# Choosing the experts of two routed layers in groups of 4 tiles, as their logits are moved, in place of 16 tiles at a time

## What is computed

```python
xn = _layernorm(x)
s = _L0_attn_ref(xn, ...)            # gated linear attention, 4 heads, chunks of 64
g = _silu(_L0_ffn_ref(xn, ...))      # 8 experts, the best 2 of a token
x = x + s * g
xn = _layernorm(x)
s = _L1_attn_ref(xn, ...)            # softmax attention, 16 heads
g = _silu(_L1_ffn_ref(xn, ...))      # 16 experts, the best 2 of a token
x = x + s * g
```

```python
# layer 0
gate_scores = softmax(x @ Wg.T)                       # [tokens, 8]
topk_val, topk_idx = top_k(gate_scores, 2)
topk_val = topk_val / (topk_val.sum(-1) + 1e-9)
# layer 1
scores = x @ router_w + router_bias                   # [tokens, 16]
topv, topi = top_k(scores, 2)
weights = softmax(topv)
```

## Time and profile before

| | |
|---|---|
| median of 3 runs | 1166.89 us (1165.84 to 1169.87) |
| the profiled execution, its own time | 1174.48 us |
| its span in the profile | 1172.5 us |
| mean granted TensorE clock | 0.83 |
| TensorE busy | 794.8 us, 68% |
| VectorE busy | 646.4 us, 55%, 1112 instructions |
| ScalarE busy | 625.9 us, 53%, 1093 instructions |
| GpSimd busy | 479.5 us, 41%, 486 instructions |
| the chain that ended last | PE 38%, DVE 19%, ACT 13%, unknown 11%, issue 10%, POOL 6% |

### The profile page before, as it was taken

One profiled execution on the slowest core, in us unless ns is written; L12 is line 12 of the kernel. 1 busy time (PEld: TensorE's weight loads), 2 busy tenths in 40 slices (PEclk: granted clock), 3 DMA queues, 4 the chain that ended last, 5 costly groups with the idle time before them and its releaser, 6 DMA issues.

```text
span 1172.5 us, 23626 instructions
## 1 busy us (share of the span) xinstructions
PE 794.8 (68%) x8916; PEld 620.2 (53%) x8916; DVE 646.4 (55%) x1112; ACT 625.9 (53%) x1093; POOL 479.5 (41%) x486
## 2 busy tenths in 40 slices
PE   5735668999999882477821028777988788788610
PEld 3424557888888762254610015455656566666510
DVE  7574336766765233977670016755656647465355
ACT  4433336768775311464500025667668778687722
POOL 3067542233432444520037730004346646555635
PEclk9667869999999997677955559989889999899855
DMA  9511111011011113300013111201001111010052
GB/s 325 190 45 55 52 39 45 21 34 34 29 34 33 47 47 111 78 1 2 1 29 147 52 43 37 73 19 29 20 28 38 35 31 38 28 38 29 19 152 72
DMA packets 62366, 63.92 MB, mean 55 GB/s; under 512 B 7378, under 2 KB 52322, under 8 KB 62132
## 3 DMA queue, kind: packets, MB, share of 16 engines
q1 hardware_dynamic: 53300, 43.99, 12.8%
q0 software_dynamic: 8960, 18.43, 4.8%
HBM read 31.84 MB, written 30.55 MB: 53 GB/s over the span
## 4 chain that ended last, share of the span: by engine, by line
PE 38%; DVE 19%; ACT 13%; another core or an unknown queue 11%; issue 10%; POOL 6%; DMA 2%; SPq 0%; POOLq 0%; ACTq 0%; DVEq 0%
PE bank L441 5%; POOL ys L1710 4%; PE bank L656 3%; ACT arena L1110 3%; PE bank L593 3%; DVE arena L1580 2%; ACT L804 2%; PE bank L595 2%; PE bank L607 2%; PE bank L481 2%; PE bank L594 2%; PE bank L721 2%; PE bank L621 1%; PE bank L367 1%
## 5 line engine op out<-in xcount | busy, mean ns | idle before, releaser
L1710 POOL DMA_INDIRECT ys<-arena x152 | 169.8, 1117 | 203.3 <-DVE arena L1472 86.0
L1110 ACT ACTIVATE arena<-bank 128x512 f32<-128x512 f32 x192 | 99.3, 600 | 137.2 <-remote 92.1
L1694 POOL DMA_INDIRECT xs<-arena x128 | 128.4, 1003 | 62.4 <-issue 36.5
L593 PE MATMUL bank<-arena 128*128 128x128 bf16 x608 | 139.2, 236 | 19.4 <-DVE arena L1453 7.4
L595 PE MATMUL bank<-arena 128*128 128x128 bf16 x608 | 138.8, 235 | 3.8 <-issue 3.8
L1580 DVE TENSOR_REDUCE arena<-bank 128x2 bf16<-128x512 f32 (+1 forms) x192 | 119.2, 683 | 40.2 <-remote 26.2
L594 PE MATMUL bank<-arena 128*128 128x128 bf16 x608 | 136.7, 232 | 3.9 <-issue 3.9
L804 ACT ACT_TABLE_LOAD x70 | 89.8, 1283 | 1.2
L593 PEld LDWEIGHTS bank<-arena 128*128 x608 | 63.3, 104 | 37.5 <-issue 28.5
L441 PE MATMUL bank<-arena 128*128 128x256 f32 x256 | 69.1, 424 | 18.4 <-DVE arena L1359 17.2
L679 PE MATMUL bank<-arena 32*128 32x256 bf16 (+1 forms) x512 | 22.3, 263 | 86.7 <-ACT arena L1110 61.2
(11 more groups left out here) (213 smaller groups left out, 2034.5 us busy)
## 6 DMA issues: line engine op xcount, KB each, us to landing
xs<-arena SPq DMA_DIRECT2D x19, 516.0 KB, 7.7
arena<-xs SPq DMA_DIRECT2D x38, 258.0 KB, 2.8
arena<-ys SPq DMA_DIRECT2D x32, 256.0 KB, 5.2
arena<-in_MF SPq DMA_DIRECT2D x8, 512.0 KB
ys<-arena POOLq DMA_INDIRECT x152
arena<-in_x SPq DMA_DIRECT2D x8, 256.0 KB, 5.6
arena<-in_W SPq DMA_DIRECT2D x8, 256.0 KB
xs<-arena POOLq DMA_INDIRECT x128
```

What stands on the lines that cost most here:

```text
L593: mm(o, hi, b[:, 0, c4], stop=False)
L1110: act(PT[kt_][:, i, gs[0]:gs[0] + len(gs), :], bank_of["s2", b, n, i][:, :].rearrange("p (g q) -> p g q", q=w), ACT.Exp, scale=8 ** -0.5). ...
L1694: eng.indirect_dma_start(xs[l][:, :], bass.IndirectOffsetOnAxis(ap=slot_i[l][:, m:m + 1], axis=0), xrow[:, t, :], None).then_inc(rows_move ...
L1710: eng.indirect_dma_start(ys[l][:, :], bass.IndirectOffsetOnAxis(ap=yid[g % 4][:, j:j + 1], axis=0), y[:, 128 * j:128 * j + 128], None).the ...
```

## The change

`choose` works on one group of 4 tiles instead of 16, and `logits_taken` calls it after each group's logits are moved, in both layers. The scratch `cand` and `ix` shrink with it, the waits of `route` go to the eighth choice, and `spread(h)` waits for the last of the four choices that it covers. The diff's first two parts are those waits on TensorE and ScalarE, the last one that on GpSimd.

```diff
@@ -396,7 +396,7 @@
-                eng.wait_ge(*chosen[l].at(1))
+                eng.wait_ge(*chosen[l].at(NG - 1))
@@ -840,14 +840,14 @@
-                eng.wait_ge(*chosen[0].at(h, 5))
+                eng.wait_ge(*chosen[0].at(4 * h + 3, 5))
...
-                eng.wait_ge(*chosen[l].at(1))
+                eng.wait_ge(*chosen[l].at(NG - 1))
@@ -1243,20 +1243,19 @@
                         tt(L.rearrange("p (t e) -> p t e", e=E), bank_of["logits", u][:, 0:n].rearrange("p (t e) -> p t e", e=E), bc(rb, 1, sh),
                            ALU.add).then_inc(l_moved.sem, 1)
-                    if h % 4 == 3:
-                        choose(l, h // 4)
+                    choose(l, h)
 
             def choose(l, h):
 
-                E, C, Z = EXPERTS[l], chosen[l], 16 * EXPERTS[l]
-                sh = [128, 16, E]
+                E, C, Z = EXPERTS[l], chosen[l], 4 * EXPERTS[l]
+                sh = [128, 4, E]
                 L3 = RS[l]["cu"][:, Z * h:Z * h + Z].rearrange("p (t e) -> p t e", e=E)
                 cand = RS[l]["to"][:, 0:Z].rearrange("p (t e) -> p t e", e=E)
-                ix = RS[l]["ix"][:, 0:16]
+                ix = RS[l]["ix"][:, 0:4]
                 Oem = one_hot[:, 0:64 * E].rearrange("p (e k t) -> p e k t", e=E, k=2)
-                tsh = slice(16 * h, 16 * h + 16)
+                tsh = slice(4 * h, 4 * h + 4)
                 rv = bc(rev[l], 1, sh)
-                eng.wait_ge(*l_moved.at(8 * l + 4 * h + 3))
+                eng.wait_ge(*l_moved.at(8 * l + h))
```

## The result

| | before | with the change |
|---|---|---|
| median, measured side by side | 1166.37 us (1161.17 to 1169.87, 4 runs) | 1186.19 us (1181.51 to 1187.93, 4 runs) |
| the profiled execution | 1174.48 us | 1181.51 us |
| its span | 1172.5 us | 1178.5 us |
| VectorE | 646.4 us, 1112 instructions | 664.9 us, 1250 instructions |
| TensorE | 794.8 us | 797.0 us |

The ratio is 1.0167, with a 95% interval of [1.0118, 1.0217]: slower, as forecast, but by 19.8 us (13.8 to 25.3) where 6.8 was forecast, and just outside the range of 1161 to 1185.

What follows compares the result with a forecast made beforehand. It took VectorE to become Layer 0's bound and small choices to delay waiting engines in Layer 1: 2.8 + 4.0 = 6.8 us on the median of 1166.89, giving 1173.7 us, range 1161 to 1185.

Steps and rivals of the forecast that it cites:

- The price of single instructions: VectorE in both layers: a 128x32 operation about 0.19 us, the strided one-hot 0.30 us for 32 elements, 0.45 for 64.
- the two waits of TensorE: Layer 1: first L688 waits 7 us for VectorE instead of 3.8; about 4.3 us before the counts instead of 7.9.
- The second, fourth and eighth choice of Layer 1: Second adds 3.0 us, holding up ScalarE; fourth and eighth each save 3.6 as 6.91 us becomes 3.35.
- the fourth rival: Layer 1's scatter stretch falls out otherwise, attention getting more or less far: 1160 to 1167 or 1181 to 1188 us; chance 0.12.
- The first two rivals: VectorE's gaps cover the small choices, 1155 us, chance 0.10; or about half is hidden, 1164.5 us, chance 0.16.
- The third: Rival: VectorE bounds all of Layer 1's stretch too, +13.0 us there, +15.8 in all, 1183 us; chance 0.10.
- the 20 to 26 named: Sign to look for over the whole kernel: VectorE's busy time 20 to 26 us longer.
- +2.8 forecast: Layer 0: VectorE becomes the bound, each small choice taking 2.75 us, so its work ends at 54.1 instead of 51.3 us.
- +4.0 forecast: Layer 1: eight choices of 3.35 us put 11.2 us on the path and save 7.1 at the fourth and eighth.
- 1st: Layer 1's first choice: VectorE is already on the path, TensorE waiting for it, so all 3.35 us count.
- 6th and 7th: Layer 1: two choices delay the last group of maxima that TensorE's L688 needs, +3.5 us.
- +0.8 and +0.5: Layer 1's third and fifth choices: estimated TensorE cost of a score bank freed late, possible from 0 to 3.35 us.

Runs made afterwards that it cites:

- l0_only: Kernel before with eight choices of 4 tiles in Layer 0 only, Layer 1 unchanged: 1172.63 us, ratio 1.0012.
- before_third: Kernel before, its choices given by a table, nothing else changed, traced again on a later chip: 1038.60 us.
- after_again: The change again, eight choices of 4 tiles in both layers, against the kernel before on a later chip: 1047.49 us, ratio 1.0085.
- small_cover: Kernel before with eight small choices in Layer 1 only, plus idle matmuls meant for three of TensorE's waits there: 1044.08 us, ratio 1.0069.
- delay_sixth: Kernel before plus 13 unread VectorE comparisons behind Layer 1's sixth logits copy: 1038.93 us in one run, against 1037.53.
- l1_one: Kernel before with one choice of all 32 tiles in Layer 1, Layer 0 unchanged: 1032.0 us, ratio 0.9939.
- one_choice: Kernel before with one choice of all 32 tiles in each layer: 1030.02 us, ratio 0.9926.
- before_cover: Kernel before, choices unchanged, plus three and five idle matmuls meant for two of TensorE's Layer 1 waits: 1035.66 us, ratio 0.9985.
- before_again: Kernel before rewritten with a table of choices, same instructions in the same order: 1168.31 us, ratio 0.9986.

## Why the forecast was wrong

**What held.** The price of single instructions, the direction, the choice of Layer 1 as the larger part, and the two waits of TensorE. The second, fourth and eighth choice of Layer 1 came within half a microsecond. The scatter behind it is unchanged: 148.3 and 148.0 us from its first write to the first rows read back, so the fourth rival is out. The first two rivals are out too, by the ratio. The third, that VectorE is the bound in all of Layer 1's stretch, came nearer with its numbers (13.0 us there, 15.8 in all) than the forecast did, but not with its reason: VectorE is busy for 75.5 of the stretch's 105.2 us. VectorE's busy time rose by 18.5 us, under the 20 to 26 named; the forecast's 25.7 counted 138 handoffs of 0.035 us, 4.8 us, which are no busy time.

**Layer 0: +2.8 forecast; +0.9 in the first pair of traces, +3.9 against the mean of all.** VectorE was to be the bound, and is: 28.2 us busy of the 31.4 between 20.8 and 52.24, the rest mostly handoffs. L1358 came at 52.24, not at 54.1. The work beside the choices takes the 11.3 us that it was put at (11.1 and the first copy). But a small choice takes 2.50 us of the stream, not 2.75, since what follows starts while its last one-hot is still being written (L1272 at 49.10 for 0.30 us, the next copy at 49.20); only the eighth takes 2.74. The 51.3 us from which the 2.8 were counted was itself a late one: in the thirteen traces with two choices in Layer 0 the recurrence begins between 45.0 and 51.6 us, 48.2 in the mean, and the first scatter at 61.3 us in the mean; in the three with eight at 52.1 to 52.2 and at 65.2 to 65.3. So the end was put too late and counted from a late start, and that +2.8 lies between +0.9 and +3.9 is luck. l0_only's +1.4 us (-2.5 to +5.3) contradicts neither, and shows neither.

**Layer 1: +4.0 forecast, +10.0 to +10.8 measured.** This is the step that failed. Choice by choice, in us, from the two pairs of traces:

| choice | forecast | first traces | before_third, after_again |
|---|---|---|---|
| 1st | +3.35 | +4.1 | +3.6 |
| 2nd | +3.0 | +2.9 | +3.2 |
| 3rd | +0.8 | +2.5 | +3.3 |
| 4th | -3.6 | -4.1 | -3.4 |
| 5th | +0.5 | +2.1 | +1.1 |
| 6th and 7th | +3.5 | +7.0 | +6.4 |
| 8th | -3.6 | -3.6 | -3.6 |

Two terms of the forecast were too small. The first is "A choice of 3.35 us does not quite fit into one or two of these gaps; I put +0.8 and +0.5". In the third interval TensorE is busy all the time before (14.65 of 14.65 us) and never waits for VectorE. After, it waits 0.9 us, about the +0.8 that was put, and takes 16.23 us for the same 174 matmuls: 1.6 us more, which no term had. (In the second pair it waits 1.95 us and takes 1.3 more.) The second term is that of the sixth and seventh choice, worked out with the matmuls' times taken over from the trace of before. small_cover, whose clock is 1.00 in both intervals, separates what VectorE costs from what the clock costs there: 9.28 and 13.66 us against 6.88 and 12.26 are +3.8, the forecast's 3.5. At the clocks of the uncovered traces (0.81 and 0.80, or 0.69 and 0.89) it is +6.4 to +7.0. So the size of VectorE's part was right there, and some 3 us of slower matmuls were missing in these two alone.

That the clock takes part is shown by delay_sixth, by l1_one and one_choice, and by the intervals behind the idle matmuls. How much of the 6 to 7 us that the forecast lacks is the clock's over the whole stretch is not settled: over the stretch the same matmuls take 7.4 and 9.2 us more in the two pairs, but part of that lies beside other waits. small_cover gave some 3.7 us of the stretch back and before_cover nothing, with a batch of matmuls that stood behind the wait; no time of a whole kernel shows the gain.

The Trainium skill (TensorE: Matmul & The Clock Gate, the section on a second HAM failure mode) describes, for another kernel, short idle times between groups of matmuls that keep the clock changing between its two levels. The rows above agree, with 0.62 to 0.89 where TensorE is interrupted; the forecast did not use it.

**The whole.** The change was timed at +19.8 us (13.8 to 25.3, 4 runs against 4) and at +8.9 (6.4 to 11.2, 6 runs against 12). Layer 0's 3.9 and Layer 1's 10.5 by the traces make 14.4, inside the first interval and above the second; the single layers, timed by themselves, make 1.4 + 10.9 = 12.3, between the two. The traces don't settle it. Of the first pair, 0.1 us differ until Layer 0's output is read, 10.7 from there to L404, and 4.8 less behind L404, 6.0 in all; that trace of the change is its shortest run. Of before_third and after_again it is 8.3 us until Layer 0's output is read, then 10.0, and 1.8 less behind L404. What is the same in both is Layer 1's 10 to 11 us; how much Layer 0 adds by the time that its output is read stays open, and so does the difference between +8.9 and +19.8.

## What to carry to other kernels

Splitting work on an engine that another one waits for cost twice here: the fixed part of each instruction (some 160 ns here), and the pace of the engine that is interrupted, so a forecast must not take that engine's durations over from the trace before. Where all of the results are needed only at the end, make them there in one piece, even if the piece stands on the path: in one pair of traces 6.9 us less in the middle were worth 10.6, and 4.8 more at the end cost 4.8. Compare stages between traces rather than totals, and several traces of each kernel where a granted clock or a start varies: Layer 0's recurrence began 6.5 us apart with the same instructions. And look in the trace whether work meant to fill a wait lies in it: the five idle matmuls came behind the wait that they should have filled.

## What was not expected of the hardware

The same 174 matmuls of the fifth interval took 12.2 us of TensorE at a granted clock of 1.00, 13.6 at 0.88 and 14.7 at 0.81, and with identical instructions the third ran at 0.85 in one trace and 0.82 in another. A delay of 1.85 us of VectorE was enough to lower the clock of the next 20 us of matmuls from 1.00 to 0.85 and cost 4.4 us.

The chips differ by far more than anything here. The kernel before took 1166.37 us in the first runs, 1170.67 us on the chip of before_again and 1036.66 to 1038.60 us on four others. In Layer 1's scatter, 148 us pass between the first indirect write and the first rows read back in the first traces, with one unexplained wait of 67 us, and 86 us in before_third, where the chain has no such wait and goes through GpSimd's writes themselves (59 to 76% of it, read in three pieces from 560 to 647 us). In Layer 0 the first to the last scatter take 106 and 91 us. Why is open; ratios between kernels were taken only within a chip.
